# Two heads' row scores side by side in the row halves of the array, and a new order of the units

## The reference

```python
q      = einsum('bld,dhk->blhk', x, Wq)            # 16 heads of 64
latent = einsum('bld,dc->blc', x, Wkv_down)        # 64 wide
k, v   = latent @ Wk_up, latent @ Wv_up
attn   = softmax(where(mask, q.k / 8, min))
x      = layernorm(x + einsum('bhqk,bkhd,hdo->bqo', attn, v, Wout))
...                                                # top-1 router, 32 experts, silu(g) * u, down
x      = layernorm(x + gated expert output)
```

## Time and profile before

| | before |
|---|---|
| median of the runs | 2505.95 us |
| the profiled execution's own time | 2510.11 us |
| its span, first to last instruction | 2508.0 us |
| mean granted TensorE clock | 0.967 |
| TensorE matmul busy | 2345.6 us (94%) |
| VectorE busy | 1602.7 us (64%) |
| GpSimd busy | 1678.9 us (67%) |
| ScalarE busy | 1015.1 us (40%) |

### The profile page before, as it was taken

One profiled execution on the slowest core, in us unless ns is written; L12 is line 12 of the kernel. 1 busy time (PEld: TensorE's weight loads), 2 busy tenths in 40 slices (PEclk: granted clock), 3 DMA queues, 4 the chain that ended last, 5 costly groups with the idle time before them and its releaser, 6 DMA issues.

```text
span 2508.0 us, 36804 instructions
## 1 busy us (share of the span) xinstructions
PE 2345.6 (94%) x11528; PEld 1517.6 (61%) x11528; DVE 1602.7 (64%) x4618; ACT 1015.1 (40%) x1992; POOL 1678.9 (67%) x1623
## 2 busy tenths in 40 slices
PE   6999999999999999999999999999999999949996
PEld 4555575556655665566555665566556655537774
DVE  4677657765676667765776567666776577335553
ACT  3445424443444334542444334433444344212222
POOL 1688756975787757875797568766787579623444
PEclk8999999999999999999999999999999999969998
DMA  3222100200011001100020001100110001224652
GB/s 87 60 64 81 39 14 14 73 18 14 18 49 37 18 10 39 47 18 13 18 69 18 14 18 51 35 18 9 43 43 18 18 14 55 68 79 155 193 180 68
DMA packets 96818, 118.96 MB, mean 47 GB/s; under 512 B 12289, under 2 KB 75783, under 8 KB 96625
## 3 DMA queue, kind: packets, MB, share of 16 engines
q1 hardware_dynamic: 89712, 99.98, 14.5%
q0 software_dynamic: 6912, 16.64, 1.9%
HBM read 46.91 MB, written 37.90 MB: 34 GB/s over the span
## 4 chain that ended last, share of the span: by engine, by line
PE 76%; DVE 13%; issue 6%; POOL 1%; ACT 1%; DMA 0%; DVEq 0%; SPq 0%; POOLq 0%; ACTq 0%
PE value_ps L722 18%; PE misc_ps L744 9%; PE turned_ps L699 9%; PE turned_ps L702 8%; PE misc_ps L621 8%; PE turned_ps L891 6%; PE row_ps L674 6%; PE turned_ps L674 3%; PE misc_ps L734 3%; DVE masked_row L1117 2%; DVE q_hl L1098 2%; DVE q_hl L1097 2%; DVE rinv L1151 1%; PE misc_ps L770 1%; DVE x L1199 1%
## 5 line engine op out<-in xcount | busy, mean ns | idle before, releaser
L964 ACT ACTIVATE probs<-turned_ps 128x512 f32<-128x512 f32 (+2 forms) x1280 | 652.1, 554 | 815.2 <-PE turned_ps L702 801.2
L504 POOL TENSOR_TENSOR half_sums<-half_sums,probs 128x1024 f32<-128x1024 f32 (+3 forms) x512 | 832.4, 1626 | 33.2 <-ACT probs L964 15.9
L722 PE MATMUL value_ps<-probs,lat_keys 128*64 128x512 f32 (+3 forms) x3072 | 597.7, 511 | 0.0
L699 PE MATMUL turned_ps<-q_hl,lat_hi 128*128 128x512 f32 (+2 forms) x1280 | 529.7, 414 | 1.5 <-ACT fold_v L1009 1.5
L702 PE MATMUL turned_ps<-q_max,lat_lo 65*128 65x512 f32 (+2 forms) x1280 | 483.7, 378 | 2.5 <-DMA q_max<-both_rows 2.5
L479 POOL TENSOR_SCALAR_AFFINE_SELECT probs<-probs 128x256 f32<-128x256 f32 x512 | 210.3, 411 | 405.0 <-ACT probs L964 404.1
L1117 DVE CUSTOM_DVE_ANT_0 masked_row<-row_ps,future 128x512 bf16<-128x512 f32 (+4 forms) x707 | 347.3, 511 | 189.6 <-PE row_ps L674 184.2
L499 POOL TENSOR_TENSOR half_sums<-probs 128x768 f32<-128x768 f32 (+1 forms) x128 | 269.4, 2105 | 140.8 <-ACT probs L964 118.2
L674 PE MATMUL row_ps<-lat_hi,q_hl 128*128 128x512 f32 (+4 forms) x1026 | 324.3, 356 | 33.0 <-DVE neg_max L1117 18.5
L722 PEld LDWEIGHTS value_ps<-probs,lat_keys 128*64 128x64 f32 x3072 | 190.5, 139 | 265.3 <-issue 199.8
L699 PEld LDWEIGHTS turned_ps<-q_hl,lat_hi 128*128 128x128 f32 x1280 | 244.6, 191 | 137.3 <-issue 107.9
(11 more groups left out here) (191 smaller groups left out, 2652.3 us busy)
## 6 DMA issues: line engine op xcount, KB each, us to landing
q_max<-q_hl SPq DMA_DIRECT2D x256, 128.0 KB
slots_x<-router SPq DMA_DIRECT2D x8, 1290.0 KB, 6.0
ex_x<-slots_x SPq DMA_DIRECT2D x64, 129.0 KB, 2.4
x_in<-in_L_attn_x_bld SPq DMA_DIRECT2D x8, 1024.0 KB, 5.5
layer_out<-x_in SPq DMA_DIRECT2D x8, 1024.0 KB, 4.5
ex_w<-in_L_ffn_w_gate SPq DMA_DIRECT2D x32, 256.0 KB, 3.7
ex_w<-in_L_ffn_w_up SPq DMA_DIRECT2D x32, 256.0 KB, 3.8
ex_w<-in_L_ffn_w_down SPq DMA_DIRECT2D x32, 256.0 KB, 4.3
```

Source lines behind the costliest of these rows:

```text
L504: nc.gpsimd.tensor_tensor(total, total, now[:, :, q0:BANK], ALU.add).then_inc(added, 1)
L699: nc.tensor.matmul(scores_of(n, h), lat_hi[b % 2][:, keys], q_hl[gp % 2][:, heads, cols], start=True, stop=False)
L722: mm = nc.tensor.matmul(value_ps[h * LD:(h + 1) * LD, q0:BANK], lat_keys[b % 2][:, j, :], probs[:, n % NPROBS, h, q0:BANK], start=(j == 0) ...
L964: nc.scalar.activation(probs[:, n % NPROBS, heads, q0:BANK], scores_of(n, h), ACT.Exp).then_inc(exp_done, 1)
```

## The change

For the pairs from the second on, in slots with t even, a unit's matmul uses only the head's half of the partitions: the high part of the queries (64 rows) against the latent's copy in the same half. The two units of such a slot so stand in the two row halves of the array and write different banks. In the other slots the matmul stays as it was. The order of the units is new: the widths are now 512, 128, 384, 256, 512, 320, 512, 320, 512, 256, 512, 384, so that the six even slots hold 512 five times and 384 once. `normalise` on VectorE is written with a list of tiles; it issues the same instructions in the same order, with waits that are already met.

```diff
-    UNITS = ([(h, i, 0) for i in range(HPB) for h in range(2)]
-             + [(h, i, k) for i in range(HPB, NT) for k in range(2) for h in range(2)])
+    UNITS = [(h, i, k) for i, k in ((3, 0), (0, 0), (2, 0), (1, 0), (5, 0), (4, 0), (6, 0), (4, 1), (7, 0), (5, 1), (7, 1), (6, 1))
+             for h in range(2)]
...
+    in_row_half = lambda gp, u: gp > 0 and u // 2 % 2 == 0
...
-                nc.tensor.matmul(dst[:, 0:k1 - k0], q_hl[gp % 2][:, h, i * P:(i + 1) * P], lat_hi[b % 2][:, k0:k1],
+                rows = slice(h * LD, (h + 1) * LD) if in_row_half(gp, u) else slice(0, P)
+                nc.tensor.matmul(dst[:, 0:k1 - k0], q_hl[gp % 2][rows, h, i * P:(i + 1) * P], lat_hi[b % 2][rows, k0:k1],
                                  start=True, stop=True).then_inc(rows_full, 1)
...
-            def normalise(b, hf):
-                dve.wait_ge(rstd_ready, b * 2 + hf + 1)
-                for i in range(hf * HPB, (hf + 1) * HPB):
+            def normalise(b, tiles):
+                for i in tiles:
+                    dve.wait_ge(rstd_ready, b * 2 + i // HPB + 1)
                     last = nc.vector.tensor_scalar(x1[:, i, 0:D], x1[:, i, 0:D], mean_var[:, i, 0:1], rstd[:, i:i + 1],
                                                    ALU.subtract, ALU.mult)
-                last.then_inc(x1_ready, 1)
+                    if i % HPB == HPB - 1:
+                        last.then_inc(x1_ready, 1)
```

More of the change, by code:

```diff
@@ L284, in build_layer @@
             if b and p == 2:
-                for use, t in zip([(hf, kd) for hf in range(2) for kd in range(KD)], (3, 5, 7, 10)):
+                for use, t in zip([(hf, kd) for hf in range(2) for kd in range(KD)],
+                                  (3, 5, 7, 10)):
                     late[t].append(("x1T", b - 1, *use))
@@ L1308, in _ @@
                     if b and (p, t) in ((1, 10), (2, 4)):
-                        normalise(b - 1, p - 1)
+                        normalise(b - 1, range((p - 1) * HPB, p * HPB))
             for use in ENDING:
@@ L1321, in _ @@
                 if use[0] == "rest" and use[2] == NT - 1:
-                    normalise(LAST, 0)
+                    normalise(LAST, range(HPB))
                     variance(LAST, 1)
-                    normalise(LAST, 1)
+                    normalise(LAST, range(HPB, NT))
             def copy_rows(e):
```

## The result

The changed kernel takes 2532.66 us (median of 4 runs, 2531.78 to 2534.63). The kernel before, run beside it, takes 2506.59 us (4 runs, 2505.47 to 2508.99). The ratio is 1.0101, with a 95% interval of 1.0087 to 1.0114: slower by 26 us. The forecast was 2510 us with a range of 2472 to 2541. So the time lies in the range, the sign is the one that had the highest chance (slower, 0.42), and the middle is 23 us too low.

A forecast was written before the change was run, and what follows sets the result against it. TensorE was taken as the bound, matmuls busy 94% of the span, with waits for VectorE. Terms -4 - 2 + 2 + 10 - 2 = +4 us on the profiled 2510.11 gave 2514, or 2510 us median; range 2472 to 2541.

The forecast's parts named there:

- slower, 0.42: Sign for the whole kernel: a measured time above the kernel before, given chance 0.42, against same 0.27 and faster 0.31.
- The price of a change of shape and of a bare load: TensorE, even slots: each array shape change costs 0.08 to 0.09 us, then an unhidden weight load costs 0.10.
- The first rival: Even slots: the 64-row load or shape change hides behind the running matmul, saving 38 or 34 us; 2472 or 2476; chance 0.19.
- Side by side: Even slots: both halves' streams and loads overlap, the second half lagging 0.02 us, bounded by 0 and 0.048.
- the second rival: Even slots: the two loads go one behind the other, second stream 0.08 later, 30 us in all; 2540; chance 0.09.
- Slot 4: Its value product starts 0.22 us later, against 0.17 without waits; 0.05 more in 44 pairs, 2 us.
- Slot 8: Its value product is 0.53 us late, against 0.20 without waits; 0.33 more in about 30 pairs, 10 us.
- the sum without waits: TensorE's steps for a pair, leaving out waits: 4.84 us before, 4.78 after; 4 us less in 63 pairs.
- Plain pairs: Pairs without batch work: one takes 27.6 us after the change, 27.4 before.
- Pairs with batch work: The 0.06 us saving was taken for all 63 pairs; slot 11 gives back 0.26 in 7 pairs, 2 us.
- The fourth rival: The order relieves VectorE and both plain-pair waits, in slots 4 and 8, vanish: -6 - 18.5 - 9, 2472; chance 0.05.
- pays for itself, some new waiting: Main case for the whole kernel: the edit pays for itself, some us of new waiting, 2498 to 2523; chance 0.60.

The follow-up runs named there:

- Experiment 3: Changed kernel with both heads' units of an even slot in the same row half; 2583.68 us, ratio 1.0299 to the kernel before.
- experiment 8: Changed kernel with row halves in the odd slots in place of the even; 2575.71 us, ratio 1.0267 to the kernel before.
- Experiment 1: Changed kernel with the new order kept and every unit at full height; 2524.84 us, ratio 1.0062 to the kernel before.
- experiment 4: Changed kernel with row halves only in slots 0, 6 and 10, new order kept; 2525.09 us, ratio 1.0064 to the kernel before.
- 2: Changed kernel with the unit order of the kernel before, row halves kept in even slots; 2534.05 us, ratio 1.0099 to the kernel before.
- experiment 5: Changed kernel at full height, with 128-key units in slot 0 and 512 in slot 1; 2511.62 us, ratio 1.001 to the kernel before.
- 9: Experiment 5 with row halves added in slots 2, 4, 6, 8 and 10; 2530.34 us, ratio 1.0084 to the kernel before.
- 6: Changed kernel at full height, reordered with 128-key units in slot 2 and 256 in slot 6; 2499.25 us, ratio 0.9955 to the kernel before.
- 7: Experiment 6 with row halves added in slots 8 and 10 only; 2492.57 us, ratio 0.9937 to the kernel before.
- 10: Experiment 7 with widths 256, 512, 128, 384 in slots 0 to 3; 2492.42 us, ratio 0.9924 to the kernel before.

## Why the prediction was right and where it was wrong

**The price of a change of shape and of a bare load: right.** 0.09 and 0.10 were predicted, 0.095 and 0.10 measured (0.33 less 0.235; 0.43 less a step of 0.235 and 0.095). Experiment 3 shows both again, in steps of 0.33 in a row. That each even slot has three changes and a load that doesn't hide held in all slots, odd ones in experiment 8 too. The first rival, a hidden load or change, is out. The rule of the Trainium skill (TensorE: Matmul & The Clock Gate, Part 3) that the prediction held against it, a load overlaps matmuls in flight only in other array rows, does not fit these traces, though, and the measurement decides: at full height the loads hide behind a stream in the same rows (step of 0.235), and in experiment 3 one does at half height. Only across a change of shape is the load bare.

**Side by side: right.** A lag of 0.02 was taken, between 0 and 0.048. The starts are 0.003 us apart in slot 0 and 0.006 in slot 10. The Trainium skill's rule (TensorE: Matmul & The Clock Gate, Part 3) of about 4 ns for a further tile agrees with it. The loads run side by side as well. Timeline of the weight loads in slot 0:

```profile
1023.72 0.19 PEld L679 LDWEIGHTS row_ps<-lat_hi,q_hl 64*128 64x128 f32 x2 [0.37 <-issue]
```

Two loads of 128 columns in 0.19, as long as a single one's record. So the second rival is out too. An even slot with 512 columns costs 0.52 above its plain step, where 0.55 was before and 0.535 predicted.

**Slot 4: right, and nearly to the number.** The value product was to start 0.22 us later after the pair's start. It starts at 9.95 (1032.65 less 1022.70), before at 9.74: 0.21. The working was right too. VectorE in slots 3 and 4:

```profile
1031.01 0.69 DVE L1103 TENSOR_TENSOR q_hl<-misc_ps,q_hl 64x512 fp32r<-64x512 f32 x1
...
1031.74 0.42 DVE L1122 CUSTOM_DVE_ANT_0 masked_row<-row_ps,future 128x256 bf16<-128x256 f32 x1
```

`low_q` starts 0.39 us later after the pair's start than in the earlier trace rows (8.31 for 7.92; 0.21 + 0.20 was the working), the narrower unit gives 0.27 back, and slot 4's first unit goes when `low_q` is done, its second when the first unit of slot 3 is. Experiment 1 shows the halves' share. With the order alone the value product starts at 9.85, so about half of the 0.21 is the order's and half the halves'.

**Slot 8: right in kind, too large.** Its value product was to be 0.53 us late, 0.33 beyond the sum without waits. It starts at 19.60 in place of 19.23, so 0.37. From its first unit to the value product slot 8 takes 1.01, where 0.43 is without a wait; before it took 0.97, where 0.565 is. So the wait grew by 0.17 in 27 pairs, and the slot by 0.13 us, 3.5 us in all for the 10 of the sum. The step that was too large is the delay of VectorE's chain, 0.22 and 0.20 added up whole. VectorE after, for the earlier trace rows:

```profile
1038.21 1.29 DVE L1126 TENSOR_REDUCE unit_max<-row_ps 128x1 f32<-128x512 f32 x2 [0.62 <-PE row_ps L679]
1039.42 0.27 DVE L1137 CAST both_rows<-misc_ps 8x128 fp32r<-8x128 f32 x1
```

The chain does begin 0.40 later after the pair's start (15.51 for 15.11), but `both_rows` only 0.31 (16.72 for 16.41). The prediction read 1026.34 and 1026.35 as no gap. In this trace `both_rows` starts 0.08 before the end of the record ahead of it, so before there was a pause of 0.09 that could take delay up. It was a wait for the transposed maxima, whose matmul (L684) ends at 1026.24. So before the chain to slot 8 began at that matmul, and only with the halves in slot 6 do the maxima come last (in experiment 4 too, not in 1). The wider unit of slot 7 then adds 0.07, not 0.09.

**Plain pairs: 27.6 predicted, 27.49 measured.** The slots without slot 8 came out within 0.04 us each of their terms; slot 8's 0.13 in place of some 0.3 is the difference. Up to here the prediction erred to the slow side.

**Pairs with batch work: the step that failed.** The sum took the plain pair's savings over into all 63 pairs and held only the waits of plain pairs against them. Its sentence that the new wide units of slot 0 "lie beside the value products of 1.7 us" looked at TensorE and not at what is queued behind these units on VectorE. Two waits for the bank `misc_ps` were missed.

First, slot 3 of pairs 1, 2 and 6, where the slot's late work is not a plain pair's and needs that bank. VectorE empties it with `low_q`, behind the maxima of slot 2. The matmuls of slot 3 in pair 1 of batch 4, before and after:

```profile
1145.36 0.64 PE L674 MATMUL row_ps<-lat_hi,q_hl 128*128 128x512 f32 x2
1146.66 1.13 PE L744 MATMUL misc_ps<-fold_v,headsT 128*128 128x256 f32 x4 [0.67 <-DVE q_hl L1098]
```

```profile
1159.34 0.40 PE L679 MATMUL row_ps<-lat_hi,q_hl 128*128 128x256 f32 x2
1160.82 1.35 PE L749 MATMUL misc_ps<-fold_v,headsT 128*128 128x256 f32 x5 [1.08 <-DVE q_hl L1103]
```

The narrower units come out 0.24 us sooner, and this only makes the wait longer; the 0.17 by which slot 2's maxima start later comes on top. So where 0.23 were counted as gained, 0.17 is lost: 0.40 in 21 pairs, 8.4 us, which is the growth of the three waits from 14.2 to 22.7. Slot 4 is then 0.07 to 0.08 cheaper than in a plain pair, so 6.7 us net. Experiments 1 and 2 split it: with the order alone the three waits are 6.3 us each and slot 3 has -0.01 to 0, so the 0.23 are lost; with the halves alone it has +0.17.

Second, slot 1 of pair 4, shown in experiment 5: +0.48 over a plain pair's slot 1, 3.4 us in 7 batches. (In single batches it is more, 0.57 to 0.67 in three; in two others the slot was long before as well.)

Slot 0 of pair 3 has +0.21 over a plain pair's too, 1.5 us, and it goes with slot 0 narrow (0.00 in experiment 5, +0.51 in 1). But nothing waits for `both_rows` there. This slot runs mostly at the half clock, 37.4 us in 8 batches and 30.0 before, and there the wide units cost about twice the 0.26 of the other pairs. It is a price of the order at the lower clock.

Then there is what slots 8 to 11 give back. In plain pairs their sum is -0.18, in pair 6 +0.13. Narrower units bring nothing in its slots 9 and 11, for a reason that was not traced, and in its slot 10 a matmul waits for `misc_ps` behind `low_q` as in slot 3: 6.9 us in 7 pairs, before 5.8. Over pairs 0, 1, 2, 3 and 6 this makes 0.34 us a batch, some 2.4 us. That pair 3's slot 11 would give back 0.26 in 7 batches did not come: it has +0.14.

Together: 5.7 (0.09 in 63 pairs) + 6.7 + 3.4 + 1.5 + 2.4 = 19.7 of the 22.4 us of the loop. The rest, 2.7, is in single long slots that the medians leave out. All of the added half clock is in the pairs that have them: 4.8 us in pair 2, 8.8 in pair 3 and 3.4 in pair 4. So the clock can make it, but no run isolates it.

**The clock.** The prediction took it as it was. In the loop the trace before has 81.9 us at the half clock in 16 stretches and the one after 99.0 in 19. They begin in pair 0's slot 3, pair 2's slots 6 and 11, and the first slots of pairs 3 and 4. After, pair 4 of batch 4; windows with the columns of the earlier trace rows:

```profile
1262.00:1266.00 4.00, 2.24 (x12) 1.33 (x10) 3.93 (x10) 0.72 (x2) 4.00 (x4) 1.00 0.30 66
1266.21:1269.62 3.41, 3.41 (x10) 0.76 (x8) 3.34 (x8) 0.54 (x2) 3.41 (x4) 0.52 0.01 2
```

The granted clock falls from 1.00 to 0.52, 2.4 to 1.2 GHz, after 4 us in which the matmuls were busy for 2.24. So a wait that is made longer may be paid again in the clock. If TensorE was the bound in all of the 17 us more, they cost 8.5 us; since some fall into slots that wait anyway, this is an upper end. Pair 2 moved with it by 6 us between experiments 1 and 5 and by 10 between 5 and 9 (28.2, 15.8 and 38.0 us at the half clock). No experiment set the clock apart from the waits, and which wait will bring a stretch of half clock on, as in pair 2's slots 6 and 7 in experiments 1, 6 and 9, stays open.

**The fourth rival, relief, which had 0.05.** It did not happen with this order, for the reason given against it: the chains start in slots 2 and 6, whose widths stayed. With exactly those two narrowed (experiments 6, 7 and 10) half of it happens: slot 4's wait goes nearly whole, slot 8's stays, as its chain did not begin at slot 6's maxima. The runs are 10 to 16 us faster, a third to a half of the 34 that the rival promised.

**The chances.** Slower had 0.42 and the likeliest case "pays for itself, some new waiting" ended at 2523, 10 us short of the result. The range held the time only because it reached to the rival with the loads in turn (2540), which was wrong itself, so that the time lies in the range is luck. So is part of the sign: the forecast's own sum was +4 us, no change within what a measurement tells. No case stood for the pairs with batch work.

## What to carry to other kernels

Halving the rows of a short matmul buys one stream and pays for a change of shape and a bare load: here 0.235 against 0.095 and 0.10 for 512 columns, and a loss of 0.02 at 384; and it puts the first result off by 0.2 us, which is lost where the next engine's late chain starts from it. When units change places, follow on the receiving engine whatever stands behind them in its queue, in each kind of iteration and not in the plain one alone: the plain pair had 0.09 us of change here, the pairs with batch work up to 0.7. The gain was in the order, by putting narrow units where the late chain to slot 4 begins; the same at slot 6 brought nothing, because the chain to slot 8 began at TensorE's own transpose and not at slot 6's maxima.

## What the runs showed of the hardware

- Two half-height matmuls in opposite row halves start 3 ns apart and their loads, 128 columns each, go side by side in the 0.19 us of one record. In the same half they follow after 0.33 us, bare load and stream; the second load is hidden behind the first stream there (it starts 0.11 after the first), as at full height, where the step is 0.235.
- A change of shape costs 0.095 us and a bare load 0.10 in both directions, for 128 to 64 rows, 64 rows to 64 columns and 64 to 128 rows alike, with 320 and 512 columns.
- A second half that waits for its bank loses the overlap whole: 0.47 and 0.58 us in slots 4 and 8 in place of 0.003.
- The loop spent 78.5 to 119.5 us at the half clock, in 15 to 22 stretches, over the twelve kernels, all with nearly the same instructions in other orders or places of the array. At the half clock slot 0 of pair 3 took 5.34 us in one batch where it took 2.98 at the full clock in the next.
